# A graph-attention stage inside a long kernel: lists rounded to 8 columns, the partly filled block behind the loops, and loops nested four pairs at a time

## The reference

```python
h = (x_flat @ W_gat).reshape(M, HEADS, NUM_EXPERTS)          # M = 8192 tokens, 4 heads x 4
src = jnp.concatenate([edge_index[0], loops])                # indices drawn from 0..16383
dst = jnp.concatenate([edge_index[1], loops])
e = jax.nn.leaky_relu(a_src[src] + a_dst[dst], negative_slope=0.2)
e_max = jax.ops.segment_max(e, dst, num_segments=M)
ee = jnp.exp(e - e_max[dst])
denom = jax.ops.segment_sum(ee, dst, num_segments=M)
alpha = ee / (denom[dst] + 1e-16)
agg = jax.ops.segment_sum(h[src] * alpha[:, :, None], dst, num_segments=M)...
```

## Time and profile before

| | us |
|---|---|
| median of 3 runs (lowest, highest) | 2666.33 (2662.26, 2668.05) |
| the profiled execution, its own time | 2675.84 |
| its span | 2674.0 |
| busy in the span: PE, DVE, ACT, POOL | 1372.7, 1413.1, 637.2, 820.0 |
| gathers of L1861 | x544, 535.0 busy |

### The profile page before, as it was taken

The page is one execution under the profiler, slowest core; times in us unless marked ns, Lnnn a source line. Parts: engine busy times, 40 slices in busy tenths (PEclk is TensorE's granted clock), DMA queues, the critical chain, the costliest instruction groups (busy, mean ns, idle before and its releaser), DMA issues.

```text
span 2674.0 us, 19577 instructions
## 1 busy us (share of the span) xinstructions
PE 1372.7 (51%) x6758; PEld 604.7 (23%) x6758; DVE 1413.1 (53%) x2047; ACT 637.2 (24%) x1015; POOL 820.0 (31%) x870
## 2 busy tenths in 40 slices
PE   2636422388861000000000005879967999978989
PEld 1433311332340000000000001234533222224432
DVE  7999999956545301101101116655136556567556
ACT  1301200066110000000000004532025666620043
POOL 1000000077337877777777766000000000000000
PEclk8667655589875555555555556989968999989989
DMA  9200000000015111111111110010000000000000
GB/s 396 116 1 1 0 0 0 21 14 14 22 15 24 57 18 20 20 14 20 20 14 20 20 14 9 1 25 0 1 1 4 1 1 1 1 7 0 0 1 32
DMA packets 62635, 63.00 MB, mean 24 GB/s; under 512 B 42820, under 2 KB 56532, under 8 KB 60116
## 3 DMA queue, kind: packets, MB, share of 16 engines
q1 hardware_dynamic: 36532, 52.16, 6.7%
q0 software_dynamic: 26016, 9.69, 3.9%
HBM read 21.68 MB, written 40.11 MB: 23 GB/s over the span
## 4 chain that ended last, share of the span: by engine, by line
PE 32%; POOL 27%; DVE 25%; issue 12%; ACT 1%; DMA 0%; POOLq 0%; DVEq 0%; SPq 0%; ACTq 0%
POOL rows L1861 19%; DVE keys L2124 13%; PE bank L890 9%; PE bank L520 7%; PE bank L557 7%; POOL keys L2006 5%; POOL scratch_start L1853 2%; PE bank L457 2%; DVE x_pair L1428 2%; PE bank L425 2%; PE bank L542 2%; POOL wide L1876 1%; DVE keys L2122 1%; PE bank L553 1%; DVE wide L463 1%
## 5 line engine op out<-in xcount | busy, mean ns | idle before, releaser
L1861 POOL DMA_INDIRECT rows<-scratch_row,idx_ring x544 | 535.0, 983 | 165.7 <-issue 165.7
L806 DVE TENSOR_TENSOR hid<-hid,bank 128x512 f32<-128x512 f32 (+1 forms) x320 | 272.9, 894 | 218.8 <-PE bank L542 217.0
L1510 PE MATMUL bank<-ident,last 128*20 128x128 f32 x3 | 0.8, 410 | 741.3 <-DVEq L1707 741.3
L2124 DVE TENSOR_TENSOR keys<-keys 128x1024 f32<-128x1024 f32 (+1 forms) x388 | 353.3, 952 | 7.3
L656 ACT ACTIVATE hid<-bank,weights_odd 128x512 f32<-128x512 f32 x448 | 281.2, 685 | 176.4 <-PE bank L520 174.8
L1675 DVE COPY idx_ring<-src_i 128x32 int32 (+1 forms) x17 | 3.3, 196 | 548.3 <-DMA rows<-scratch_row,idx_ring 548.2
L520 PE MATMUL bank<-wide,weights_odd 64*128 64x512 f32 x896 | 272.4, 691 | 17.6 <-ACT hid L656 17.5
L557 PE MATMUL bank<-hid,weights_odd 128*64 128x512 f32 x896 | 244.5, 626 | 0.5 <-DVE hid L806 0.5
L842 POOL MEMSET wide<- 128x132 f32 (+2 forms) x3 | 1.0, 333 | 703.9 <-DVEq L1129 336.2
L2006 POOL DMA_INDIRECT keys<-scratch_sorted,weights_odd x128 | 123.5, 965 | 221.2 <-DVEq L2177 179.7
L890 PE MATMUL bank<-wide,weights_even 128*128 128x512 f32 x416 | 186.3, 603 | 1.5 <-issue 1.5
(11 more groups left out here) (416 smaller groups left out, 2023.9 us busy)
## 6 DMA issues: line engine op xcount, KB each, us to landing
scratch_sums<-wide SPq DMA_DIRECT2D x12, 2048.0 KB, 35.8
rows<-scratch_row,idx_ring POOLq DMA_INDIRECT x544, 2.4
scratch_sums<-sums SPq DMA_DIRECT2D x17, 384.0 KB, 2.6
scratch_start<-wide SPq DMA_DIRECT2D x2, 2048.0 KB, 9.3
a_dst_e<-scratch_start SPq DMA_DIRECT2D x1, 4096.0 KB, 13.1
keys<-scratch_sorted,weights_odd POOLq DMA_INDIRECT x136, 2.7
x_pair<-in_x SPq DMA_DIRECT2D x1, 2048.0 KB, 8.2
edge_i<-in_L_ffn_edge_index SPq DMA_DIRECT2D x1, 2048.0 KB, 13.1
```

The lines of the kernel that those rows point to most:

```text
L806: v.tensor_tensor(blocks, blocks, bank[4 + b][:, :].unsqueeze(1).broadcast_to([P, KS, 512]), ALU.mult).then_inc(S("scaled"), 1)
L1861: g.indirect_dma_start(out=rows[:, b, c, :], out_offset=None, in_=row_d[:, :], in_offset=at(idx_ring[:, b, c:c + 1])).then_inc(s_gath[b], 16)
L2124: m = v.tensor_tensor(o, p, q, op)
```

## The change

1. **Lists rounded to 8 columns.** The number of columns is now counted in steps of 8 (`PART`) instead of 32: four limits for each block, one for each of its quarters. A block all of whose quarters are needed is full; one more block may be partly filled, with 1 to 3 quarters (`blocks_i[6]`). The list length `span[:, 0:1]` is 8 times the quarters.
2. **The partly filled block behind the loops.** GpSimd and VectorE run their loops over full blocks only. GpSimd then gathers 8, 16 or 24 columns of the last block, and VectorE works all 32 columns of it after waiting for those. Columns behind the list's end hold old rows: `same` is set to 1 there, and NEG is added to `a_dst_e` there, with `behind_end`, by one operation over all columns from the third block on. ScalarE and SyncE still run over all blocks in use, the partly filled one included.
3. **Loops nested.** `rounds` runs pairs up to 3 as before, then an outer loop over seven groups of four pairs, each skipped as a whole if its first pair isn't in use.

```diff
+FEW = 4
+PART = 8
...
-            with eng.Fori(first, NW // 2) as i:
+            rounds(eng, first, used, body)
+            return used
+
+        def rounds(eng, first, used, body):
+
+            with eng.Fori(first, FEW) as i:
                 for b in range(2):
                     with eng.If(i < used[b]):
                         body(i, b)
-            return used
+            with eng.Fori(1, NW // 2 // FEW) as o:
+                with eng.If(o * FEW < used[0]):
+                    with eng.Fori(0, FEW) as k:
+                        i = eng.snap(o * FEW + k)
+                        for b in range(2):
+                            with eng.If(i < used[b]):
+                                body(i, b)
...
+            link(v.tensor_scalar(behind_end, col_iota, span[:, 0:1], NEG, ALU.is_ge, ALU.mult))
...
+            link(v.scalar_tensor_tensor(same[:, :], col_iota, span[:, 0:1], same[:, :], ALU.is_ge, ALU.max))
...
-            link(v.tensor_scalar(limits, list_w, float(WIN * P), None, ALU.mult))
-            link(v.memset(limits[:, 0:2], -1.0))
+            for q in range(4):
+                link(v.tensor_scalar(limits[:, q, :], list_w, float(WIN * P), float(q * PART * P), ALU.mult, ALU.add))
+            link(v.memset(limits[:, :, 0:2], -1.0))
             link(v.tensor_scalar(limits, limits, total, None, ALU.is_lt))
-            link(v.tensor_reduce(span[:, 1:2], limits, AX, ALU.add))
-            link(v.tensor_reduce(span[:, 2:4], limits.rearrange("p (i b) -> p b i", b=2), AX, ALU.add))
-            link(v.tensor_copy(blocks_i[:, 0:2], span[:, 2:4]))
-            link(v.tensor_copy(blocks_i[:, 2:3], span[:, 1:2]))
+            link(v.tensor_reduce(block_f[:, 7:8], limits.rearrange("p q w -> p (q w)"), AX, ALU.add))
+            for q, at in ((0, 0), (3, 3)):
+                link(v.tensor_reduce(block_f[:, at:at + 2], limits[:, q, :].rearrange("p (i b) -> p b i", b=2), AX, ALU.add))
+                link(v.tensor_reduce(block_f[:, at + 2:at + 3], limits[:, q, :], AX, ALU.add))
+            link(v.tensor_scalar(span[:, 0:1], block_f[:, 7:8], float(PART), None, ALU.mult))
+            link(v.scalar_tensor_tensor(block_f[:, 6:7], block_f[:, 5:6], -4.0, block_f[:, 7:8], ALU.mult, ALU.add))
+            link(v.tensor_scalar(block_f[:, 7:8], block_f[:, 6:7], float(16 * PART), None, ALU.mult))
+            link(v.tensor_tensor(block_f[:, 8:10], block_f[:, 0:2], block_f[:, 3:5], ALU.subtract))
+            link(v.tensor_scalar(block_f[:, 10:11], block_f[:, 5:6], -1.0, None, ALU.add))
+            link(v.tensor_copy(blocks_i[:, :], block_f))
             v.sem_inc(S("pairs"), 1)
...
-            link(v.tensor_scalar(span[:, 0:1], span[:, 1:2], float(WIN), None, ALU.mult))
...
-            each_block(v, 1, window)
+                window(b, b, (s_gath[b], 16 * WIN), True)
+            rest = a_dst_e[:, 2 * WIN:, :]
+            link(v.tensor_tensor(rest, rest, behind_end[:, 2 * WIN:].unsqueeze(2).broadcast_to([P, EPP - 2 * WIN, HEADS]), ALU.add))
+            full = full_blocks(v)
+            rounds(v, 1, full, lambda i, b: window(2 * i + b, b, (s_gath[b], (i + 1) * (16 * WIN))))
+            split = split_block(v)
+            for b in range(2):
+                with v.If(split[b] > 0):
+                    part_rows = v.value_load(blocks_i[0:1, 7:8], min_val=16 * PART, max_val=16 * WIN)
+                    g = v.value_load(blocks_i[0:1, 5:6], min_val=2, max_val=NW - 1)
+                    window(g, b, (S("s3_part_rows"), part_rows))
...
-            used = each_block(g, 1, next_gather)
+            full = full_blocks(g)
+            rounds(g, 1, full, next_gather)
+            split = split_block(g)
+            parts = g.value_load(blocks_i[0:1, 6:7], min_val=0, max_val=3)
+            for b in range(2):
+                with g.If(split[b] > 0):
+                    before = g.value_load(blocks_i[0:1, 10:11], min_val=1, max_val=NW)
+                    g.wait_ge(S("s3_idx_next"), before)
+                    g.wait_ge(S("s3_msg"), before)
+                    g.sem_inc(S("s3_pool_go"), 1)
+                    gather_part(b, 0)
+                    with g.If(parts > 1):
+                        gather_part(b, 1)
+                    with g.If(parts > 2):
+                        gather_part(b, 2)
+            used = blocks_in_use(g)
```

More of the change, by code:

```diff
@@ L83, in program @@
         span = sb("span", [P, 4])
-        blocks_i = sb("blocks_i", [P, 3], I32)
+        blocks_i = sb("blocks_i", [P, 11], I32)
         W = {}
@@ L221, in program @@
         spec_n = spare(NT)
-        limits = spare(NW)
+        limits = spare(4 * NW).rearrange("p (q w) -> p q w", q=4)
+        block_f = spare(11)
         list_w = spare(NW)
@@ L1491, in each_block, with full_blocks, split_block @@
                         body(i, b)
-            return used
+            with eng.Fori(1, NW // 2 // FEW) as o:
[5 more added lines that the diff above has]
+                                body(i, b)
+        def full_blocks(eng):
+            eng.wait_ge(S("pairs"), 1)
+            return [eng.value_load(blocks_i[0:1, 3 + b:4 + b], min_val=1, max_val=NW // 2) for b in range(2)]
+        def split_block(eng):
+            return [eng.value_load(blocks_i[0:1, 8 + b:9 + b], min_val=0, max_val=1) for b in range(2)]
         col_iota = chan_mem[:, TOK // 2:TOK // 2 + EPP]
         list_of = chan_mem[:, TOK // 2:TOK].bitcast(BF16)
+        behind_end = wide[:, TOK + NT * C:TOK + NT * C + EPP // 2].bitcast(BF16)
         list_rows = tok_mem[0:NT, :].bitcast(BF16)
@@ L1602, in places_vector @@
+            link(v.tensor_copy(blocks_i[:, :], block_f))
             v.sem_inc(S("pairs"), 1)
-            link(v.tensor_scalar(span[:, 0:1], iota_p, span[:, 1:2], None, ALU.mult))
-            link(v.tensor_scalar(list_f, list_r, span[:, 0:1], None, ALU.add))
-            link(v.tensor_scalar(list_i, list_f, float(WIN), None, ALU.mult))
+            link(v.tensor_scalar(span[:, 1:2], iota_p, span[:, 0:1], None, ALU.mult))
+            link(v.tensor_scalar(list_f, list_r, float(WIN), span[:, 1:2], ALU.mult, ALU.add))
@@ L1607, in places_vector @@
+            link(v.tensor_copy(list_i, list_f))
             v.sem_inc(S("list_at"), 1)
-            link(v.tensor_scalar(span[:, 0:1], span[:, 1:2], float(WIN), None, ALU.mult))
             link(v.reciprocal(span[:, 1:2], span[:, 0:1]))
@@ L1663, in flat, with window @@
                 return t.rearrange("p f w -> p (f w)")
-            def window(i, b, first=False):
-                g = 2 * i + b
+            def window(g, b, rows_in, first=False):
                 nth = g + 1 if first else v.snap(g + 1)
@@ L1673, in step @@
                     v.wait_ge(S(name), nth)
-                v.wait_ge(s_gath[b], (i + 1) * (16 * WIN))
+                v.wait_ge(*rows_in)
                 step("s3_idx_next", v.tensor_copy(idx_ring[:, b, :], src_i[:, bass.ds((g + 2) * WIN, WIN)]))
@@ L1694, in graph_vector @@
             for b in range(2):
-                window(0, b, True)
-            each_block(v, 1, window)
+                window(b, b, (s_gath[b], 16 * WIN), True)
[9 more added lines that the diff above has]
+                    window(g, b, (S("s3_part_rows"), part_rows))
             all_blocks = v.value_load(blocks_i[0:1, 2:3], min_val=2, max_val=NW)
@@ L1861, in gather, with gather_part @@
                     g.indirect_dma_start(out=rows[:, b, c, :], out_offset=None, in_=row_d[:, :], in_offset=at(idx_ring[:, b, c:c + 1])).then_inc(s_gath[b], 16)
+            def gather_part(b, q):
+                for c in range(q * PART, (q + 1) * PART):
+                    g.indirect_dma_start(out=rows[:, b, c, :], out_offset=None, in_=row_d[:, :], in_offset=at(idx_ring[:, b, c:c + 1])).then_inc(S("s3_part_rows"), 16)
             gather(0)
```

## The result

| | before | after |
|---|---|---|
| median, us (lowest, highest; 6 runs each) | 2663.43 (2662.26, 2668.05) | 2654.22 (2652.03, 2662.18) |
| ratio | | 0.9961, 95% interval 0.9948 to 0.9975 |
| gathers of rows | 544 | 512 + 8 |

The changed kernel is faster by 0.39%, about 10 us (7 to 14). The forecast was 2648.6, with 62% on 2644 to 2653, and with 2639 to 2661 as the range that takes in both bounds of the masking. The time, 2654.2, lies outside the first and inside the second; the gain is some 60% of the forecast 17.7 us. The forecast stood on the median of three runs, 2666.33; that of all six is 2663.43, and these 2.9 us bring the time nearer to the forecast than the gain is, which is luck.

The account below looks back on a forecast made before the run. GpSimd's row gathers, 1.25 us each, were taken to set the pace. Terms -30.0 + 7.6 + 1.7 + 2.5 + 0.5 = -17.7 us from 2666.33 gave 2648.6 us, range 2644 to 2653 (62%).

Parts of the forecast that it names:

- both bounds of the masking: Masking's cost to GpSimd's gathers: from below 0, as under L1644; from above +18.1 us, at L1688's rate.
- 1. 24 gathers less: Last block in GpSimd's gather stage: 8 gathers in place of 32, 1.25 us each, -30.0 us.
- 2. masking beside the gathers: VectorE's 8.4 us operation on a_dst_e behind block 1 holds up a GpSimd gather: +7.6 us.
- 3. operations in the lists: Two more VectorE operations over 2048 columns in lists_vector hold up GpSimd's scatters: +1.7 us.
- 4. places: Chain of small VectorE operations from L1595, on the path: 17 in place of seven, one dropped; +2.5 us.
- 5. from the loops to the last block: Six skipped groups and register reads ahead of the last block's gathers and window: +0.5 us, between 0 and 5.
- 6. VectorE's quick exit: VectorE's 17.35 us behind the loop nearly vanish, worth 0; rival that it is on the path: up to 17 us, 2%.
- the rival that the masking is free: Mask operation costs GpSimd's gathers nothing: -25.3 us in all, 2641 us; 14%.
- the one of L1688's rate: Mask operation runs at L1688's slow rate: 10.5 us more lost, -7.2 us in all, 2659 us; 12%.
- The fetches: Rival: nested loops force instruction fetches of some 3 us, 2670 to 2691 us; within 0.2% of before 5%, slower 4%.
- VectorE's margin of 4.4 us: Between VectorE free at 6.9 and the last 8 columns landed at 11.3, to cover skipping and four register reads.
- The bound of 5 us: Upper limit of the cost from the loops to the last block, forecast at +0.5 us.

Follow-up runs that it names:

- mask in the last block: Changed kernel, but the mask is added to a_dst_e only in the partly filled block's 32 columns; 0.9922 of the kernel before.
- nesting alone: The kernel before with the nested loops of the diff and nothing else; ratio 1.0003 to the kernel before.
- whole blocks: Changed kernel with a block's four limits all equal: 17 full blocks, 544 gathers, no partly filled block; 1.0059 of the kernel before.
- extra matmuls: 16 matmuls in TensorE's idle time ahead of stage 3's experts; against the kernel before: changed kernel 0.9947 and 0.9948, kernel before with them 0.9983.
- flat loops: Changed kernel with the earlier unnested loop over 32 pairs, partly filled block still behind it; 0.9990 of the kernel before.
- registers read ahead: Changed kernel with the mask in the last block only and VectorE's four register reads moved ahead of the loops; 0.9922 of the kernel before.
- smaller mask: Changed kernel with same and a_dst_e masked only in the last block's 32 columns, registers read ahead; 0.9908 of the kernel before, median 2650.60 us.

## Why the prediction was right or wrong

| term | forecast, us | measured in the profile, us |
|---|---|---|
| 1. 24 gathers less | -30.0 | -30.0 |
| 2. masking beside the gathers | +7.6 | +7.4 |
| 3. operations in the lists | +1.7 | +3.1 |
| 4. places | +2.5 | +2.3 |
| 5. from the loops to the last block | +0.5 | +2.5 |
| 6. VectorE's quick exit | 0 | +0.6 |
| sum up to the merge | -17.7 | -14.1 |
| not placed: the measured gain is 10, 5 and 10 us | 0 | +4, +10, +4 (not settled) |

**Right.** The bound, the count of columns (65,720 edges, 512 + 8 gathers), and the step that decides the size: an operation of VectorE that isn't late and has 34 us of cover still costs GpSimd its whole length less 1 us. In the profile the experiment with the mask in the last block gives these 7.4 us back. So falls the rival that the masking is free, and the one of L1688's rate: 8.42 us was forecast as 8.4. The fetches are not there: GpSimd's waits on L1901 are 156.0 us over 512 gathers, 0.305 each, and the queue of instructions moved the same 54 packets and 0.88 MB as in the earlier trace rows. The quick exit is worth nothing, as the run with the nesting alone shows.

**Mis-sized.** Step 3: the rate of L1573 (0.47 us lost per us) was one scatter's luck; the two new operations and their neighbour L1598 each hold a scatter that starts within 0.4 us of their own start, while before it started 1.1 us behind that of L1573. Step 5: I priced six skipped groups at up to 4.5 us, and they took 4.7, but "four register reads" stood in the same sentence with no price, and they took 2.4. VectorE's margin of 4.4 us held only the first. The bound of 5 us held.

**What stays open** is what happened to the other 4 to 10 us, for the terms that can be read from the profiles make 14.1. The prediction took the stages behind the graph as unchanged, with "since the terms are differences, I carry them over". Their code is unchanged, their time in the profiles isn't. From the merge to the end of the span, kernels with the old block schedule take 1051.3, 1040.6, 1043.3 and 1042.7 us (before twice, nesting alone, whole blocks), mean 1044.5; those with a partly filled block and no extra matmuls 1047.3, 1053.8, 1054.2, 1052.8, 1051.4, 1050.2 and 1053.9, mean 1051.9. The two places where they differ are stretches in which TensorE is near full and its clock is low for a shorter or longer time. With the merge 14.4 us earlier (mean of five profiles with the changed kernel's schedule against four of before's) and 7.4 given back this makes -7 us, beside the measured -10, -5 and -10.

But the run times don't bear this out as the cause. If every kernel with a partly filled block lost these 7 us, the others should miss their terms too:

| kernel | terms from the profiles, us | by the ratio, us (95% interval) |
|---|---|---|
| the changed kernel | -14.1 | -10, -5, -10 (each give or take 4) |
| flat loops | -1 | -3 (-6 to +1) |
| mask in the last block | -21.0 | -21 (-27 to -15) |
| registers read ahead | -23.5 | -21 (-26 to -15) |
| smaller mask | -26.5 | -25 (-30 to -19) |

With 7 us more the terms of flat loops and of the mask in the last block would lie outside their intervals. And with the extra matmuls in both kernels, 9 us of difference remain in place of 14. So by the run times the shortfall shows in the changed kernel itself, with or without the extra matmuls, and not in its variants; its cause isn't shown, and the intervals are too wide to rule out that a part of it is chance. That a longer low stretch costs time of this size is shown within profiles (65.6 or 72.5 us; 159.1 or 165.8). Why the clock rises later in kernels with a partly filled block is open as well. TensorE is idle for 45 us ahead of the experts there, against some 28 before, but nesting alone has 39 and rose early, and the second place lies 340 us further on.

## What to carry to other kernels

Where GpSimd's indirect DMAs set the pace, count each long VectorE operation with two inputs in on-chip memory (SBUF) at its full length on GpSimd's path, however idle VectorE is, and cut it to the columns that need it: here that was worth 7.4 us, beside some 8 us for the whole change. A block moved behind a loop puts everything between the two (skipped rounds, register reads) on the path, so read registers ahead and bound the loop closely. And stages whose code is unchanged can take another time: sum the profile on both sides of the edited stage, in more than one execution, and hold the sum against the run times of every variant, before a difference of 0.3% is explained.

## What the runs showed of the hardware that wasn't expected

- A skipped round costs the same 0.73 to 0.78 us on VectorE whether it holds one If or two, and reading a register from on-chip memory 0.6 us (four reads moved ahead of the loops: 7.14 us of way became 4.74).
- GpSimd's gap ahead of the last 8 gathers is the usual 0.30 us with six skipped groups and four register reads in it, and 6.25 us with 24 skipped pairs in place of the groups. It prepares the former under gathers already issued, and all but 6 us of the latter.
- A tensor_scalar of 2048 elements from f32 to bf16 takes 1.28 us and holds a scatter up like a two-input operation does (+0.63 us).
- One execution of the same kernel differs from the next by up to 21 us (2658.6 to 2679.7), and most of what could be placed is how long TensorE's clock stays low in two stretches: 7 us in the one (65.6 or 72.5), and in the other 1.4 us for the kernel before (161.4 or 162.8) and 2.5 for the changed kernel with extra matmuls (159.1 or 161.6).
